# Attention value products issued in two runs of four pieces per step instead of six short runs, in an adaLN attention + mixture-of-experts kernel

## The reference

```python
h = layernorm(x) * (1 + ca) + sa          # sa, ca, ga, sb, cb, gb come from silu(c) @ wmod
x = x + ga * attn(h)                      # 16 heads of 8 channels, band |i - j| <= 128
h = layernorm(x) * (1 + cb) + sb
x = x + gb * moe(h)                       # 8 experts, top 2 of each token, silu(h w1) * (h w3) @ w2
```

## Time and profile before

| what | value |
|---|---|
| median of 3 runs | 331.8 us (330.05, 331.8, 332.74) |
| span of the profiled execution | 336.7 us |
| time of the profiled execution around its span | not recorded apart from the span |
| PE busy | 279.1 us (83%) |
| DVE, ACT, POOL busy | 217.2 (65%), 183.2 (54%), 160.2 us (48%) |
| mean granted TensorE clock | 0.923 |
| PV matmuls (L1350) | 512 records, 39.3 us of PE's busy time |
| attention steps 1 to 8 | 36.3 to about 184 us |

### The profile page before, as it was taken

The page is one execution under the profiler, slowest core; times in us unless marked ns, Lnnn a source line. Parts: engine busy times, 40 slices in busy tenths (PEclk is TensorE's granted clock), DMA queues, the critical chain, the costliest instruction groups (busy, mean ns, idle before and its releaser), DMA issues. The chain is left out here.

```text
span 336.7 us, 7278 instructions
## 1 busy us (share of the span) xinstructions
PE 279.1 (83%) x2264; PEld 203.3 (60%) x2264; DVE 217.2 (65%) x552; ACT 183.2 (54%) x393; POOL 160.2 (48%) x252
## 2 busy tenths in 40 slices
PE   3558799999999898999798498776999999999700
PEld 2134354555554545454343397776999999999700
DVE  4678879788889789999945648562433333333136
ACT  7432476767776575666654364334566666665400
POOL 4050236255756579696958544635333333333400
PEclk9958899999999999999958789959999999999965
DMA  3842231342526262490112333333355544455365
GB/s 95 175 75 65 65 111 43 96 154 60 209 61 197 71 202 78 102 193 11 42 31 72 97 85 112 104 103 110 105 149 142 144 142 143 141 142 137 95 207 174
DMA packets 57254, 38.22 MB, mean 114 GB/s; under 512 B 5240, under 2 KB 52104, under 8 KB 57216
## 3 DMA queue, kind: packets, MB, share of 16 engines
q1 hardware_dynamic: 52880, 31.16, 34.0%
q0 software_dynamic: 2272, 4.69, 4.2%
q10 hardware_dynamic: 2064, 1.91, 2.1%
HBM read 23.58 MB, written 6.75 MB: 90 GB/s over the span
## 5 line engine op out<-in xcount | busy, mean ns | idle before, releaser
L480 ACT ACTIVATE probs<-psB 128x512 f32<-128x512 f32 x128 | 71.2, 594 | 26.6 <-PE psB L1330 25.0
L913 DVE TENSOR_REDUCE negm<-psA 128x4 f32<-128x1024 f32 x64 | 77.6, 1221 | 11.7 <-PE psA L1308 11.1
L1478 PE MATMUL psA<-qs,kd 128*128 128x128 f32 x624 | 79.6, 283 | 6.2 <-ACT qs L562 6.2
L1478 PEld LDWEIGHTS psA<-qs,kd 128*128 128x128 f32 x624 | 76.3, 200 | 6.6 <-ACT qs L562 6.6
L771 POOL DMA_INDIRECT y_d<-ys,qs x39 | 37.7, 967 | 72.1 <-ACT ys L552 68.6
L1173 DVE TENSOR_TENSOR qs<-psA,kd 128x512 f32<-128x512 f32 x39 | 27.0, 692 | 55.4 <-PE psA L1478 33.3
L643 POOL TENSOR_SCALAR_AFFINE_SELECT probs<-probs 128x512 f32<-128x512 f32 x64 | 39.3, 639 | 35.8 <-ACT probs L480 35.6
L1305 PE MATMUL psA<-kd,qs 96*128 96x512 bf16 x128 | 48.2, 400 | 2.0 <-DVE negm L913 1.5
L1330 PE MATMUL psB<-qs,kd 98*128 98x256 bf16 x256 | 46.9, 282 | 0.5 <-ACT probs L480 0.2
L1488 PE MATMUL psB<-kd,qs 128*128 128x128 f32 x312 | 42.5, 280 | 1.0 <-ACT ys L552 0.6
L1350 PE MATMUL psO<-probs,vx 128*32 128x256 f32 x512 | 39.3, 407 | 1.2 <-POOL probs L643 1.2
(11 more groups left out here) (187 smaller groups left out, 331.5 us busy)
## 6 DMA issues: line engine op xcount, KB each, us to landing
kd<-in_L_ffn_experts_w_dram SPq DMA_DIRECT2D x39, 256.0 KB
w_sb<-in_L_ffn_experts_w_dram SPq DMA_DIRECT2D x8, 512.0 KB
kd<-parts SPq DMA_DIRECT2D x96, 32.0 KB
qs<-parts SPq DMA_DIRECT2D x42, 64.0 KB
mod_sb<-mod_d SPq DMA_DIRECT2D x8, 320.0 KB, 5.0
qs<-xs_d SPq DMA_DIRECT2D x39, 65.0 KB
pay<-pay SPq DMA_DIRECT2D x8, 128.0 KB
probs<-y_d SPq DMA_DIRECT2D x3, 256.0 KB, 4.5
```

What stands on the lines that cost most here:

```text
L480: nc.scalar.activation(probs[:, kt, n % PRING], psB[:, kt, :].rearrange("p (h q) -> p h q", h=H2), ACT.Exp).then_inc(s["exped"], 1)
L913: nc.vector.tensor_reduce(negm[:, b % 2, :, :, j], psA[:, n % 2].rearrange("p q (h k) -> p q h k", h=H2), AX.X, ALU.max, negate=True).then ...
L1478: last = nc.tensor.matmul(ps[:, k * P:(k + 1) * P], w[:, r, k * P:(k + 1) * P], xsT[:, r], start=True, stop=True)
```

## The change

The calls of `weigh_values` in PE's loop are moved. Before, half 0 of the batch is issued at j = 5 (pieces 0 and 1), j = 6 (piece 2) and j = 7 (piece 3), and half 1 of the batch before it at j = 1 (piece 4), j = 2 (pieces 5 and 6) and j = 3 (piece 7). After, all four pieces of half 0 stand at j = 6 and all four of half 1 at j = 2, each time behind the second part of `scores_B`. The last half of the last batch, behind the loop, was already in one run and stays. No instruction is added or taken away, and no other engine's program is changed; the waits on `masked`, `v_ready` and `o_ready` move with pieces 0 and 4.

```diff
@@ -1445,11 +1445,11 @@
                         h2_T(step - 3)
                     if has(prev):
                         scores_B(prev, j, 1)
-                    for i in {5: (0, 1), 6: (2,), 7: (3,)}.get(j, ()):
-                        if has(prev):
+                    if j == 6 and has(prev):
+                        for i in range(4):
                             weigh_values(prev, i)
-                    for i in {1: (4,), 2: (5, 6), 3: (7,)}.get(j, ()):
-                        if has(prev - 1):
+                    if j == 2 and has(prev - 1):
+                        for i in range(4, 8):
                             weigh_values(prev - 1, i)
```

## The result

The kernel after takes 342.6 us (median of 4 runs, 342.06 to 342.84) against 332.27 us (4 runs, 330.05 to 333.17): a ratio of 1.031, 95% interval 1.025 to 1.037, so 10.3 us slower where 8.5 was forecast; the time itself was forecast as 340.3. Between experiments the kernel before had medians of 332.5 to 333.8 us; each experiment is compared with the runs beside it, and a difference in us is its ratio times about 333.

The account below looks back on a forecast made before the run. The prediction took late scores of pairs 3 and 7 reaching DVE and ACT as the bound, not PE's work. Its step terms summed to 8.5 us on 331.8, giving 340.3 us, range 332.5 to 344.8.

Parts of the forecast that it names:

- What bounds the kernel: From pair 3 on, when scores of pairs 3 and 7 reach DVE and ACT counts, not PE's amount of work.
- Point 1: j = 1, piece 4 gone: `project_qk` starts 0.2 us earlier in steps 2 to 5, no gain in steps 6 and 7.
- Point 2: j = 2, four pieces instead of two: scores of pair 3 come 0.86 us later, `row_max` 4 +0.7, `o_T` +0.86.
- Point 3: j = 5, two pieces gone: PE early at `scores_B` 6 waits for ACT; +1.2 in step 1, +0.4 in steps 2 and 3.
- Point 4: j = 6, four pieces: scores of pair 7 1.29 us later behind `logits`; almost hidden in step 5, +0.9 in step 4.
- PE's waits: Forecast sign: PE's idle time grows from 0.54 to about 1.6 us before `logits`, 0.78 to about 1.4 before `xn_T`.
- Step 8: At the low clock, +1.2 us at the last `exps`; bounds -0.9 and +2.5, the latter if both moved runs meet that clock.
- Steps 6 and 7: Forecast terms: step 6 +0.85 + 0.2, step 7 +0.85; in the table +1.05 each for 5-6 and 6-7.
- rival C: More PE idle around step 8 keeps the low clock for two more runs: 343.7 us, chance 0.10.
- A: Drains from entering and leaving PV runs decide; 5.7 us of PE time saved gives 326.1 us, chance 0.12.
- B: A draw: pair 3's lateness is made up within the step, leaving steps 1, 4 and 8; 334.3 us, chance 0.16.

Follow-up runs that it names:

- free place at j = 6 of step 5: Kernel before with the scores_A products of pair 6 computed twice in steps 4 to 7, no piece moved: ratio 1.010, +3.2 us.
- added scores of pair 3: Kernel before with the scores_A products of pair 3 computed twice in steps 2 to 7, no piece moved: ratio 1.010, +3.4 us.
- half 1 kernel: Kernel before with only half 1 issued in one run of four at j = 2, half 0 still spread: ratio 1.020, +6.7 us.
- Half 0 alone: Kernel before with only half 0 issued in one run of four at j = 6, half 1 still spread: ratio 1.014, +4.7 us.
- kernel with the run at j = 7: Kernel before with half 0 in one run of four at j = 7, behind the scores of pair 7, half 1 spread: ratio 1.015, +5.1 us.
- second profile of the kernel before: Kernel before run again with unchanged code for another profile: ratio 1.000, span 331.9 us.
- kernel with half 0 at 5 and 7: Kernel before with half 0 in two runs of two pieces at j = 5 and j = 7, half 1 unchanged: ratio 0.991, 3.0 us faster.
- the filled kernel: Kernel after with scores_A of pair 6 (steps 4 to 7) and pair 1 (steps 6, 7) computed twice: 1.024, +7.9 us against the kernel before.
- its filled form: Kernel with half 0 at 5 and 7, plus six extra unread matmuls in PE's step 8 waits: 0.996, -1.4 us against the kernel before.
- kernel with pairs of pieces: Kernel before with half 0 in pairs at j = 5 and 7 and half 1 in pairs at j = 1 and 3: ratio 1.000.

## Why the prediction came out right, point by point

The direction and the mechanism were right; that the total came so near is in part luck. Up to `logits` of step 6 the entries of the kernel after sum to 5.4 us where 6.25 was forecast, and the last two to 5.4 where 2.25 was.

- **What bounds the kernel.** Right. PE is the busiest engine, and saving its time bought nothing; both halves alone and the free place at j = 6 of step 5 agree. The added scores of pair 3 fit too, but a bound PE would have given nearly the same (+4.0), as their expectation says.
- **Point 1, piece 4 gone, -0.2.** Right in kind. Against the start of step 5 PE starts `project_qk` 0.19 us earlier (118.15 - 112.30 against 114.51 - 108.47), right behind `m_copy`, which ends at 118.09; the entries of the half 1 kernel contain it.
- **Point 2, pair 3 late.** Right. DVE's wait went from 0.92 to 1.59 us (about 1.6 was forecast), and 0.66 us of delay put there alone came back as 0.66 per step. The half 1 kernel's entries for steps 2 to 4, 0.28, 0.54 and 0.38, are below the 0.6, 0.65 and 0.5 that were expected, the first by more than half; why was not tried.
- **Point 3, PE early at `scores_B` 6.** Right, +1.22 in step 1 for 1.2.
- **Point 4, pair 7 late behind `logits`.** Right. Half 0 alone had +0.75 in step 4 for 0.9 and nothing in step 5, where DVE's slack was to hide it; with the run behind the scores of pair 7, steps 1 to 4 together fell from +2.83 to +0.45.
- **PE's waits.** At `logits` 1.73 us for about 1.6. At `xn_T` of step 5 0.89 us instead of about 1.4: there PE itself is late by the run behind `logits`, which point 4 says and the list of signs forgot.
- **Step 8, +1.2.** Mis-sized: +2.89. Two runs of four fell into the low clock there, and my sum had one; the bound for that case, +2.5, was passed too. With waits in steps 4 to 7 filled it was +1.61, and step 8 then had 6.8 us at half clock, as many as the second profile of the kernel before, instead of 13.7. But a low stretch of 13.7 us cost about 0.6 in the kernel with half 0 at 5 and 7, so that the clock makes up the difference is likely and not shown.
- **Steps 6 and 7, 1.05 each.** 5-6 was +0.77; 6-7 +2.49, of which filling the waits took back 0.97. The clock stood at half for 3.4 us there in the kernel after and not in the filled one. This is rival C at a place where I had not put it: it was to act around step 8, and it acted in step 6.
- **Rivals A and B.** A fell with the two kernels that run one half each, which have fewer drains and are slower. B needed the lateness of pair 3 to be made up within the step, and it is not made up in any.

So the late scores carry about 8.5 us of the table's 10.8, and the low clock at most the rest, as far as the filled kernel separates them; timed, the filled kernel has 7.9 of 10.3. The split is rough: the filling adds work of its own in steps 6 and 7, and that this 8.5 is the forecast's 8.5 is chance, with 0.85 less than forecast up to `logits` of step 6 and 0.9 more behind it. What stays open: what the clock costs in step 8 of the kernel after, and why the kernel with half 0 at 5 and 7 is 2.2 us shorter there (of its 3.7 in the table). That it had no low stretch is the smaller part: its filled form had 13.7 us of it and was still 1.55 us shorter.

## What to carry to other kernels

A block of work on the busiest engine is priced by who waits for what stands behind it, not by its own saving: merging runs was to save 5.7 us of PE and cost 10.3, and moving one piece behind the scores that DVE waits for, into PE's own wait, gained 1.8 us in steps 1 to 4 (3.0 in all, the rest in step 8 and unexplained). Ask of each place whether the reader is waiting already; if so, every delay counts in full, while arriving early may only meet the next hand-over, as in step 3 of the kernel with pairs of pieces. And a wait moved onto PE can cost more than its length, because the clock may fall behind it, as at `logits` of the kernel with the run at j = 7.

## What the runs showed of the hardware

- The granted clock fell to 1.2 GHz behind waits of PE inside a busy stretch. In the kernel with the run at j = 7 PE had waited 1.65 us at `logits` (and 0.30 more behind it), and 6.8 us at half clock followed; with 0.66 us of useless matmuls in the wait the clock stayed up (1.00 in the same stretch), and 4.0 us of such work in all made that kernel 5.2 us faster. The Trainium skill (TensorE: Matmul & The Clock Gate, What's actually happening) says that activity releases the throttle; these two kernels agree. A wait alone does not decide: the half 0 kernel waited 1.64 us at the same `logits`, and the clock stayed full (timeline of PE, step 5; the run of four takes 1.87 us):

```profile
127.80 0.58 PE L1402 MATMUL psM<-gate_sb,h2T 128*128 128x8 f32 x4 [1.64 <-DVE attn L937]
128.23 0.38 PE L1330 MATMUL psB<-qs,kd 98*128 98x256 bf16 x2
128.54 1.93 PE L1350 MATMUL psO<-probs,vx 128*32 128x256 f32 x32
130.41 0.44 PE L1366 MATMUL psM<-ident,attn 128*128 128x128 f32 x2
```

- At the low clock a run of four pieces takes 3.46 to 3.58 us instead of 1.86.
- In step 5 of the kernel before, a run of 32-column matmuls between 128-column ones costs 0.24 us for entering and leaving, beside 0.43 us a piece. The run of four of the kernel after fits: 1.86 us from its start to the next matmul, which is 4 x 0.43 + 0.14. Where PE waits anyway, the price adds nothing.
- In step 8, half clock for 13.7 us delayed PE by about 5 us and the first expert tile by about 0.6, since PE otherwise waited 4.67 us there for a transfer.
